# Feed-forward stage of a two-layer gated transformer: next batch's halves, rounding copies, row maximum and token scales moved in the engines' queues

## What is computed

```python
def act_quant(x):
    scale = 127.0 / jnp.clip(jnp.max(jnp.abs(x), axis=-1, keepdims=True), 1e-05)
    return jnp.clip(jnp.round(x * scale), -128, 127) / scale
...
h = bit_linear(x, w1)                       # 512 -> 2048
h = depthwise_conv1d(h.transpose(0, 2, 1), conv_w, conv_b)   # three taps along the tokens
h = h.transpose(0, 2, 1)
h = jax.nn.silu(h)
return bit_linear(h, w2)                    # 2048 -> 512
...
x = x + jnp.tanh(g_ffn[1]) * _L1_ffn_ref(_layernorm(x, axis=-1), ...)
```

## Time and profile before

| | |
|---|---|
| three timed runs | 1752.65, 1748.03, 1750.55 us, median 1750.55 |
| the profiled execution | 1744.49 us, its span 1742.6 us |
| `ffn` in the span | from 1318 us on, the steps with all three parts some 49 to 50 us each |
| mean granted TensorE clock | 0.924 of full speed |

### The profile page before, as it was taken

The page is one execution under the profiler, slowest core; times in us unless marked ns, Lnnn a source line. Parts: engine busy times, 40 slices in busy tenths (PEclk is TensorE's granted clock), DMA queues, the critical chain, the costliest instruction groups (busy, mean ns, idle before and its releaser), DMA issues. The chain is left out here.

```text
span 1742.6 us, 24837 instructions
## 1 busy us (share of the span) xinstructions
PE 1534.6 (88%) x8799; PEld 1165.4 (67%) x8828; DVE 1056.8 (61%) x1751; ACT 795.8 (46%) x1424; POOL 695.2 (40%) x642
## 2 busy tenths in 40 slices
PE   6599999999889999989999999468777789888896
PEld 5488878888668888767788888345544555555553
DVE  3467878888555652422233333368866978888775
ACT  2155555555422112113343344146766666667762
POOL 0134443444314675243322000355515765566650
PEclk9799999999989999999999999756767989999999
DMA  3133444343349999534533333596731011111012
GB/s 136 55 101 125 152 146 152 117 145 134 115 171 368 360 342 376 211 112 162 172 109 109 108 108 107 177 313 225 234 113 37 12 37 61 61 61 61 25 49 97
DMA packets 120852, 250.66 MB, mean 144 GB/s; under 512 B 15827, under 2 KB 31187, under 8 KB 118968
## 3 DMA queue, kind: packets, MB, share of 16 engines
q1 hardware_dynamic: 85384, 146.11, 25.1%
q0 software_dynamic: 17632, 66.33, 10.6%
q10 hardware_dynamic: 17744, 36.97, 5.6%
HBM read 142.41 MB, written 105.64 MB: 142 GB/s over the span
## 5 line engine op out<-in xcount | busy, mean ns | idle before, releaser
L2200 PE MATMUL f_banks<-b_xdT,w1h 128*128 128x512 f32 x640 | 194.0, 445 | 38.2 <-POOL b_xdT L1987 24.4
L206 PE MATMUL e_u_ps<-e_xs,w_shared 128*128 128x512 f32 x768 | 181.0, 396 | 8.5 <-DVE e_sg L1185 6.0
L2200 PEld LDWEIGHTS f_banks<-b_xdT,w1h 128*128 128x128 f32 x640 | 125.2, 204 | 90.3 <-issue 24.9
L206 PEld LDWEIGHTS e_u_ps<-e_xs,w_shared 128*128 128x128 f32 x768 | 146.7, 192 | 40.4 <-DVE e_sg L1185 6.1
L2000 POOL TENSOR_TENSOR b_h<-b_h,b_srow 128x512 f32<-128x512 f32 x112 | 143.0, 1323 | 48.9 <-ACT b_srow L2036 48.9
L2025 ACT ACTIVATE b_h<-b_h 128x512 f32<-128x512 f32 x128 | 87.4, 683 | 114.2 <-DVE b_h L2101 114.0
L1348 PE MATMUL e_u_ps<-e_w,e_xs 128*128 128x512 f32 x528 | 133.3, 401 | 2.0 <-DVE e_xs L1277 1.2
L2169 PE MATMUL b_o_ps<-w2q,b_h 128*128 128x512 bf16 x428 | 115.4, 395 | 4.0 <-ACT b_h L2030 1.7
L2098 DVE SCALAR_TENSOR_TENSOR b_h<-f_banks,cw,b_h 128x511 f32<-128x511 f32 x128 | 95.3, 745 | 27.6 <-ACT b_h L2019 27.5
L1348 PEld LDWEIGHTS e_u_ps<-e_w,e_xs 128*128 128x128 f32 x528 | 95.7, 188 | 23.4 <-DVE e_xs L1277 1.6
L2019 ACT ACTIVATE b_h<-f_banks,cb,cw 128x512 f32<-128x512 f32 x128 | 103.6, 817 | 8.5 <-PE f_banks L2200 7.7
(11 more groups left out here) (243 smaller groups left out, 3356.9 us busy)
## 6 DMA issues: line engine op xcount, KB each, us to landing
e_xe<-slots_in_scratch SPq DMA_DIRECT2D x69, 256.0 KB, 2.6
experts_out_scratch<-e_ye ACTq DMA_DIRECT2D x69, 256.0 KB, 2.0
xin<-in_x SPq DMA_DIRECT2D x16, 512.0 KB, 4.1
xres<-in_x SPq DMA_DIRECT2D x16, 512.0 KB, 5.2
x_scratch<-x SPq DMA_DIRECT2D x32, 256.0 KB, 2.0
xn_scratch<-xn SPq DMA_DIRECT2D x32, 256.0 KB, 2.0
xn2T_scratch<-x2T SPq DMA_DIRECT2D x16, 512.0 KB, 4.2
e_x<-x_scratch SPq DMA_DIRECT2D x32, 256.0 KB
```

Source lines behind the costliest of these rows:

```text
L206: mm = pe.matmul(n.u_ps[:, (2 * q + j) % 4], n.w_shared[q // n.KH][:, pa, at:at + P], xs[:, pb, k], start=(k == 0 and (pa, pb) == PASSES[0 ...
L2200: mm = pe.matmul(f_ps[:, v % RING], n.w1h[:, k, (c - NV) * P:(c - NV + 1) * P], xdT[:, part, k], start=(k == 0 and part == 0), stop=(k == ...
```

## The change

Four tables and places move; no arithmetic changes and no DMA is moved.

- `high(s+1, 0..3)` stand together after `silu(13)` of step s, before `middle(15)`; before, two stood ahead of `silu(15)` and two behind it, after everything else of the step. In step 0 (where tile 15 is a float tile) they stand after `silu(14)`.
- Rounding copies 13, 14 and 15 of a batch move into the next step: two behind `middle(0)`, one behind `middle(1)`. The others start at tile 7. ACT's `token_row` then stands ahead of `silu(m - 1)`.
- `half_max` becomes `part_max`: the first takes ten tiles after `taps(11)`, the second six at the end of the step.
- `token_scales` follow `taps(2)`, not `taps(1)`; `outputs(s-3, 3)` go from ahead of `taps(0)` to behind `taps(1)`; `scale_row` stands at tile 6 on PE and at tile 5 on ACT.

```diff
-        lifts = {6: (0,), 7: (1, 2), 8: (3,), 9: (4, 5), 10: (6, 7), 11: (8, 9), 12: (10, 11), 13: (12, 13), 14: (14,), 15: (15,)}
+        lifts = {7: (0,), 8: (1, 2), 9: (3, 4), 10: (5, 6), 11: (7, 8), 12: (9, 10), 13: (11, 12)}
+        late_lifts = {0: (13, 14), 1: (15,)}
+        parts = ((0, 5), (5, KF // 2))
...
                         middle(m)
+                        if f2:
+                            for r in late_lifts.get(m, ()):
+                                lift_tile(s - 2, r)
+                        if front and m == (5 if s == 0 else 1):
+                            token_row()
                         if m >= 1:
                             silu(m - 1)
...
-                        if front and m == (5 if s == 0 else 1):
-                            token_row()
-                        if quant and m == 4:
+                        if quant and m == 5:
                             scale_row()
                         if quant:
                             for r in lifts.get(m, ()):
                                 lift_tile(s - 1, r)
-                    if front:
-                        act.wait_ge(f_full, s * KF + KF - 1)
-                        high(s + 1, 0)
-                        high(s + 1, 1)
+                        if front and m == (KF - 2 if s else KF - 1):
+                            act.wait_ge(f_full, s * KF + m + 1)
+                            for k in range(KD):
+                                high(s + 1, k)
                     silu(KF - 1)
-                    if front:
-                        high(s + 1, 2)
-                        high(s + 1, 3)
                 elif quant:
+                    for m in late_lifts:
+                        for r in late_lifts[m]:
+                            lift_tile(s - 2, r)
                     scale_row()
...
-                    src = h[:, s % HB, i * KF // 4:(i + 1) * KF // 4]
+                    src = h[:, s % HB, first:end]
...
-                if s >= 3:
+                if s >= 3 and not f1:
                     outputs(s - 3, 3)
...
                         taps(m)
-                        if quant and m == 1:
+                        if s >= 3 and m == 1:
+                            outputs(s - 3, 3)
+                        if quant and m == 2:
                             token_scales()
-                        if m == 9:
-                            half_max(0)
+                        if m == 11:
+                            part_max(0)
...
-                        if quant and m == 5:
+                        if quant and m == 6:
                             scale_row()
```

More of the change, by code:

```diff
@@ L2102, in taps, with part_max @@
                                              op0=ALU.mult, op1=ALU.add).then_inc(conv_done, 1)
-                def half_max(i):
-                    dve.wait_ge(h_done, s * KF + (i + 1) * KF // 2)
+                def part_max(i):
+                    first, end = parts[i]
+                    dve.wait_ge(h_done, s * KF + 2 * end)
                     if s >= 1:
                         dve.wait_ge(amt_full, s)
-                    src = h[:, s % HB, i * KF // 4:(i + 1) * KF // 4]
+                    src = h[:, s % HB, first:end]
                     dve.tensor_reduce(am[:, i], src.rearrange("p i t w -> p t i w"), AX.XY, ALU.max,
@@ L2138, in run @@
                         token_scale(s + 1, 1)
-                    half_max(1)
+                    part_max(1)
                 elif quant:
```

## The result

| | before | after |
|---|---|---|
| median | 1750.33 us (8 runs, 1745.39 to 1759.13) | 1739.72 us (8 runs, 1733.77 to 1741.30) |
| ratio | | 0.9933, 95% interval 0.9913 to 0.9953 |
| profiled execution, its span | 1744.49, 1742.6 us | 1741.30, 1739.5 us |
| `ffn`, from its first instruction to the end of the span | 424.1 us | 413.6 us |

What follows compares the result with a forecast made beforehand. It took TensorE's late feeding with low halves between steps as the bound. Six steps gave 15.2 us, steps 0 and 1 gave 0, a lower-clock restart -1, the end +2.8: 17 us, median 1733.5, range 1724 to 1745.

Steps and rivals of the forecast that it cites:

- The seam: Between steps: high halves start 4.8 us after the first maximum, not 12.3; TensorE's wait at `up(2)` shrinks from 2.89 to 0.8.
- The period: Distance between first maxima falls from 49.5 to 47.0 us, 2.5 less; 15.2 us over six steps.
- Steps 0 and 1: Start of the stage, where VectorE and ScalarE set the pace: gain 0, bounds -2 and +2 us.
- The end: Step 7, which has no high halves: its second maximum ends earlier, and everything after hangs on it; +2.8 us.
- The maximum over ten tiles: First maximum takes 5.4 us instead of 4.32; by that alone six steps lose 6.6 us, already in the sum.
- The token row: On ScalarE, comes about 8 us earlier after the first maximum, serving only GpSimd, whose slack is large.
- The covers: Slack of moved work, such as taps(0) 0.7 us, late copies 1.1, output 0.5; costed at nothing, uncovered lateness counts every step.
- Clock: Rival: TensorE's lower clock stays at every seam, giving back 1.9 us times six, 11.4; 1744.9 us; 15%.
- Ring: Rival: TensorE only arrives earlier at full banks, its stall growing by the 2.5 us won; 1748.7 us; 9%.
- Slower by ScalarE at the scale row: Rival: ScalarE's in-order copy, cover 0.5 us, blocks on a late row; 1754.8 us, or 1760 with lower clock; 5%.
- the prediction's signs: Wrong if first maxima stay 49 us or more apart, ScalarE waits for the scale row, or clock falls at every seam.
- More: Rival: no TensorE stall remains at the first maximum, a further 11 us gained; 1722 us; 6%.

Runs made afterwards that it cites:

- f1: The change plus unused filler matmuls on TensorE, eight ahead of up(0) and two ahead of each pair of up(2), in steps 2 to 7; 1731.92 us, 0.9918 of before.
- a3: The change with the row maximum split over eight and eight tiles as before, the first after taps(9); 1727.08 us, 0.9902 of before.
- a4: The change with step 0 alone as before: maximum over eight and eight tiles, high halves two ahead of silu(15) and two behind; 1732.94 us, 0.9928 of before.
- f3: a3 plus unused filler matmuls on TensorE, two ahead of up(0) and two ahead of each pair of up(2); 1724.73 us, 0.9870 of before.
- a1: The kernel before with only the four high halves moved to their new place; 1748.43 us, 1.0017 of before.
- c1: The kernel before with the high halves in their new place and ScalarE's token row ahead of silu(0); 1739.85 us, 0.9934 of before.
- h1: a3 with all 16 rounding copies back in their own step as before; 1736.40 us, 0.9924 of before.

## Why the prediction was right, and where its sizes were off

**The seam.** Right, almost to the tenth: first half X+4.8 (forecast 4.8), GpSimd X+5.5 (5.5), `up(2)` X+6.95 (6.9), its wait 0.64 (0.8), the maxima 5.4 and 3.25 us from start to next instruction (5.4 and 3.25), the ring stall 2.19 (1.9). `up(3)` starts at X+11.9 (12.0) in the short step behind it (1511.74 against X = 1499.88), and at X+12.7 in the one read above.

**The period.** Forecast 47.0, six times a gain of 2.5: 15.2 us. Measured 46.66 to 47.01 in three steps and 48.6 in three, in all 297.3 - 286.4 = 10.9. The term that was mis-sized is the clock's. I gave it 1 us once, behind the first maximum of step 1, where the step came out at 46.66, and 15% as a rival in which it falls at every seam for 1.9 us. It fell at every second one, for 1.6, 4.8 us in all. f1 shows the cause: with the idle time filled and nothing else moved, every step from 2 on is 47.0. Which of the two fillers does it, the one in the stall or the one in `up(2)`, was not separated. On the price of low clock the simple sum holds in the change: 3.4 us at half speed is 1.7 us of work lost. It is no general price: stretches of 3.4 us cost a3's steps 0.4 and 0.7. The Trainium skill, "TensorE: Matmul & The Clock Gate", section HAM oscillation, says the clock drops at recurring long waits and not at short ones; the trace agrees in part only, since the seams of long and short steps have the same waits (2.2, 0.6, three of 0.5) and differ in the outcome.

**Steps 0 and 1.** Forecast 0, bounds -2 and +2. Measured: the first maximum of step 1 starts 5.4 us later after the stage's start, of which its new place explains 2.9. So 2.5 us are lost, just outside the bound. a4 returned 2.3 of them by undoing step 0 alone; whether the halves or the maximum there do it was not separated.

**The end.** Forecast +2.8: the second maximum of step 7 ends at 1702.25, X+11.2, where I had 11.1, so +2.7. Then some 0.5 goes back: what follows takes 37.2 us instead of 36.7.

The sum as measured: 10.9 - 2.5 + 2.7 - 0.5 = 10.6.

**The maximum over ten tiles.** I named it as the part that costs, 1.1 us a step by the prices of the earlier trace rows, 6.6 in all, and left it inside the gain. f1 against f3 gives 0.8 a step, some 4.7 for six; and with a3 against the change the whole price is 8.3 in the stage, the rest being for the most part the lower clock (the six steps together are 7.3 shorter). The Trainium skill, "Perfetto Trace Analysis", section Optimizing Scalar/DVE Operations, says that breaking up instructions that hold up other engines may let work finish sooner. These 0.8 us a step agree: the longest reduction is the part to undo. The total forecast was unharmed by this, since it had the term.

**The token row.** I wrote that its move "serves only GpSimd". That is wrong. It releases the transposes as well, and without it the early halves gain nothing: a1 against c1, 16.8 us in the stage, 1.0017 against 0.9934 of before. The forecast did not suffer only because the change makes both moves.

**The covers.** Costed at nothing each. The outputs, token scales and scale row indeed seem worth nothing in this version: c1 has none of them and h1 all (with the same maximum and copies), and both stages take 413.4 us. The copies are worth 0.2 us here and 8.2 with the short maximum, most of it by way of the clock.

**The rivals.** Clock: half true, as told. Ring: the stall did grow to 2.2, as in the forecast, but did not eat the gain. Slower by ScalarE at the scale row: the cover of 0.5 us was not quite there, ScalarE waits 0.22 us for the row in each of the three long steps and not at all in the short ones. By the letter of the prediction's signs that speaks against it; in time it is far from the 3 us that the rival needs. More: no, the stall stayed.

## What to carry to other kernels

When a wait on the path is shortened, look at once for the next instruction whose operand was late for a harmless reason; here a bank shared with an unrelated row turned from free to 2.4 us. Parts of a reordering are not additive: copies worth 0.2 us beside one edit were worth 8.2 beside another (in the stages of single executions), so test a bundle by taking each part out of the best version, not only out of the one at hand. And where a clock follows the feed, try real work in the short gaps of the busiest engine.

## What the runs showed of the hardware

In steps 1 to 6 of all these kernels the stretches at the lower clock lasted about 3.4 or about 6.8 us (sometimes two in one step). Whether a seam has one may alternate from step to step although the instructions and waits are the same: in the change 48.6 and 47.0 in turn. In before the steps of 50.0 and 49.0 alternate as well, with stretches of 6.8 us in nearly all, at different distances from X. What decides it was not found. With filler of 0.2 us matmuls into a bank that was free at that time (f1), steps 2 to 6 had no such stretch, and the stage with more instructions was the shorter one.
